# Thirty-six of 72 weight blocks, not 24, get their low part in the first FFN pass of a Mamba and LoRA-FFN layer

## The reference

```python
def lora(x, w, a, b): return x @ w.T + (x @ a.T) @ b.T
mod = (silu(c) @ wmod).reshape(1, 6, 1, -1)       # sa, ca, ga, sb, cb, gb
h = layernorm(x) * (1 + ca) + sa                  # x: 1 x 2048 x 1024, fp32
xp = h @ x_proj_w.T                               # dt_in (32), B (16), C (16)
dt = softplus(dt_in @ dt_proj_w.T + dt_proj_b)
state = exp(dt * A) * state + dt * B * h          # 16 states a channel, over 2048 steps
x = x + ga * (sum(C * state) + D * h)
h = layernorm(x) * (1 + cb) + sb
hidden = silu(lora(h, gate_w, gate_a, gate_b)) * lora(h, up_w, up_a, up_b)   # 2752 wide
x = x + gb * lora(hidden, down_w, down_a, down_b)
```

## Time and profile before

| | us |
|---|---|
| median of 3 runs (2538.43 to 2544.97) | 2539.99 |
| profiled execution | 2542.05 |
| its span, first to last instruction | 2540.3 |
| first phase, to the first matmul of an FFN block | 532.5 |
| pass of chunk 0, 532.5 to 870.7 | 338.2 |
| pass of chunk 1, 870.7 to 1216.9 | 346.2 |

### The profile page before, as it was taken

One profiled execution on the slowest core, in us unless ns is written; L12 is line 12 of the kernel. 1 busy time (PEld: TensorE's weight loads), 2 busy tenths in 40 slices (PEclk: granted clock), 3 DMA queues, 4 the chain that ended last, 5 costly groups with the idle time before them and its releaser, 6 DMA issues.

```text
span 2540.3 us, 34613 instructions
## 1 busy us (share of the span) xinstructions
PE 2139.7 (84%) x11780; PEld 1908.1 (75%) x11780; DVE 1429.3 (56%) x2091; ACT 1439.4 (57%) x2803; POOL 1535.3 (60%) x956
## 2 busy tenths in 40 slices
PE   7446665558787798888899998999989999999999
PEld 4223222257776788887899997899979999999998
DVE  1354344666676567785667775677766777221111
ACT  2554555467685567665667665567656656442332
POOL 0344544689789678676787685786676989210100
PEclk9657667579898899899999999999999999999999
DMA  7554643246776667575666665666757787687786
GB/s 282 160 175 136 229 151 105 83 155 220 243 250 216 202 244 235 198 254 187 239 204 235 227 216 192 226 216 221 236 181 235 250 270 254 216 287 260 252 274 210
DMA packets 156031, 547.89 MB, mean 216 GB/s; under 512 B 17104, under 2 KB 29648, under 8 KB 152784
## 3 DMA queue, kind: packets, MB, share of 16 engines
q1 hardware_dynamic: 155856, 545.68, 64.0%
HBM read 498.32 MB, written 47.30 MB: 215 GB/s over the span
## 4 chain that ended last, share of the span: by engine, by line
PE 49%; DVE 12%; ACT 8%; issue 7%; POOL 4%; DMA 3%; SPq 0%; DVEq 0%; ACTq 0%; POOLq 0%
PE FP L693 43%; DVE ring L1075 6%; PE FP L599 3%; DVE ring L965 2%; POOL ring L1191 2%; ACT whi L902 1%; DMA raw<-w_gu 1%; ACT sqb L872 1%; DMA lo_scratch<-wlo 1%; PE FP L717 1%; DVE FP L1052 1%; POOL y L1164 1%; ACT SC L756 1%; PE FP L656 1%; POOL wlo L1204 1%
## 5 line engine op out<-in xcount | busy, mean ns | idle before, releaser
L1191 POOL TENSOR_TENSOR ring<-ring,c_row 128x736 f32<-128x736 f32 (+2 forms) x384 | 637.0, 1659 | 512.7 <-ACT hst L770 512.2
L756 ACT ACTIVATE SC<-dtb,aneg 128x368 f32<-128x368 f32 (+2 forms) x768 | 415.2, 546 | 670.3 <-DVE ring L1075 660.5
L693 PE MATMUL FP<-xhi,whi 128*128 128x368 f32 (+2 forms) x2160 | 712.1, 330 | 96.9 <-ACT whi L902 23.6
L693 PE MATMUL FP<-xlo,whi 128*128 128x368 f32 (+2 forms) x2160 | 704.4, 326 | 0.0
L693 PE MATMUL FP<-xhi,wlo 128*128 128x368 f32 (+2 forms) x2160 | 704.4, 326 | 0.0
L1075 DVE TENSOR_TENSOR_SCAN ring<-SC,hst,ring 128x368 f32<-128x368 f32 (+1 forms) x640 | 579.8, 948 | 6.8 <-ACT SC L756 6.8
L1164 POOL TENSOR_TENSOR y<-y,ring 128x736 f32<-128x736 f32 (+1 forms) x320 | 555.1, 1735 | 13.8
L693 PEld LDWEIGHTS FP<-xhi,whi 128*128 128x128 f32 x2160 | 422.8, 196 | 109.6 <-ACT whi L902 61.2
L902 ACT ACTIVATE whi<-raw 128x1024 fp32r<-128x1024 f32 (+2 forms) x408 | 409.3, 1010 | 148.2 <-PE FP L717 71.5
L965 DVE TENSOR_TENSOR ring<-hb,SC 128x736 f32<-128x736 f32 (+2 forms) x384 | 328.5, 855 | 223.1 <-PE SC L614 210.4
L693 PE MATMUL FP<-hhi,whi 128*128 128x368 f32 (+5 forms) x1188 | 391.6, 330 | 70.5 <-POOL hlo L1212 42.9
(11 more groups left out here) (97 smaller groups left out, 2355.6 us busy)
## 6 DMA issues: line engine op xcount, KB each, us to landing
wlo<-lo_scratch SPq DMA_DIRECT2D x249, 576.0 KB, 4.3
raw<-w_gu SPq DMA_DIRECT2D x249, 512.0 KB, 4.9
raw<-w_dn SPq DMA_DIRECT2D x107, 448.0 KB, 4.1
wlo<-lo_scratch SPq DMA_DIRECT2D x91, 448.0 KB, 3.9
raw<-w_dn SPq DMA_DIRECT2D x53, 512.0 KB, 4.5
wlo<-lo_scratch SPq DMA_DIRECT2D x51, 512.0 KB, 4.0
raw<-w_gu SPq DMA_DIRECT2D x44, 576.0 KB, 4.5
lo_scratch<-wlo SPq DMA_DIRECT2D x44, 576.0 KB, 5.9
```

The costliest lines, as they stand in the source:

```text
L693: last = mm(out, w, x, start=(start and k == 0 and e == 0), stop=(stop and k == n - 1 and e == 2))
L756: A(SC[:, DA0 + a, 0:CH[c]], tile_of(dtb, c, i), ACT.Exp, scale=aneg[:, i * NS + s:i * NS + s + 1]).then_inc(a_da[a], 1)
L1191: G.tensor_tensor(buf, buf, over_pair(c_row[:, k % C_SLOTS, 0:CH[c]]), ALU.mult).then_inc(g_hc, 1)
```

## The change

One line. `OTF` was each block with u % 3 == 1, 24 of them; now it is each with an odd number, 36. Of the further lists, `PREP` falls from 48 to 36 blocks, and `with_preps` spreads these over the same stretch. Four preparations stand before group 0 of chunk 0 in place of six. By size the low parts formed in the pass were 15 of 1152 columns, 5 of 896, 3 of 1024 and 1 of 560; now they are 22, 8, 4 and 1, and 1 of 640.

```diff
-OTF = [u for u in range(NU) if u % HI_SLOTS == 1]
+OTF = [u for u in range(NU) if u % 2 == 1]
 PREP = [u for u in range(NU) if u not in OTF]
 NPREP = len(PREP)
```

## The result

The changed kernel takes 2559.74 us (median of 4 runs, 2558.97 to 2560.48) against 2539.89; the ratio is 1.0075, 95% interval 1.0057 to 1.0092. It is slower by 19.9 us where 10 were forecast, inside the range of 2532 to 2569. (2539.89 is the median of four runs of the kernel before; the table ahead of the prediction has three of them.)

What follows compares the result with a forecast made beforehand. It took a ring around each scan group to pace the first phase and POOL to bound part of the first FFN pass. The pass 18.8 us longer, first phase 9.1 shorter: net 9.7 longer, 2550 us, range 2532 to 2569.

Steps and rivals of the forecast that it cites:

- First phase: Stretch before the first FFN pass: twelve fewer prepared blocks save ScalarE copies, 9.1 us shorter (bounds 0 to 16.2).
- Among the groups: First phase, scan groups: ten fewer prepared blocks at 0.6 us each, 6.4 us with the copies to extra columns.
- Before group 0: Start of first phase: two fewer prepared blocks, each costing ScalarE its full 1.35 us, save 2.7 us.
- GpSimd's work in the pass: First FFN pass: twelve more low parts, 28.5 us of work, lengthen it by 21.2 us.
- the split by stretches: First FFN pass: added work counted whole in three full stretches (13.9 us), half in the other three (7.3 us).
- SyncE's wait: First FFN pass: a load into a slot waits for the store's landing, 35 times; 2 us in all.
- the wait falls in TensorE's slack: First FFN pass: TensorE starts a loaded unit 2.5 us later but ends it before POOL's next low part.
- Rival (c): First FFN pass: SyncE becomes the bound, deciding from a landing of about 8.3 us; 2571 us; chance 0.16.
- (a): First FFN pass: POOL's waits take in the new work, pass 5 us longer; 2536 us; chance 0.24.
- (b): First FFN pass: TensorE keeps its clock through shorter waits, giving 6 us; 2526 us; chance 0.13.
- Pass 1: Second FFN pass: the later passes hold the same instructions before and after, so no term was given.
- The marks: Signs in the profile: first unit about 523 us, pass 350 to 365, POOL above 88% busy, 35 SyncE waits.

Runs made afterwards that it cites:

- e6: Kernel before with every fourth block's low part formed in the first FFN pass (18 blocks), three slots; 2543.72 us.
- e9: Kernel before with every fourth block's low part formed in the first FFN pass (18) and four slots for low parts; 2517.01 us.
- e7: Kernel before with every sixth block's low part formed in the first FFN pass (12 blocks), three slots; 2542.10 us.
- e12: Kernel before with every sixth block's low part formed in the first FFN pass (12) and four slots for low parts; 2520.25 us.
- e11: Changed kernel with three prepared low parts on VectorE in place of four, the fourth going to GpSimd; 2559.75 us in a single execution.
- e3: Changed kernel whose first-pass stores read a constant tile, so no load waits for a store's landing; 2546.07 us.
- e2: Kernel before with its 24 low parts of the first FFN pass formed over 16 columns only; 2521.79 us.
- e5: Changed kernel with first-pass low parts formed over 16 columns only and their stores reading a constant tile; 2511.79 us.

## Why the prediction was right and where it wasn't

**First phase: -9.1 us forecast, -9.3 measured, with both parts wrong, so the agreement is luck.** Among the groups ten blocks fewer were to give 6.4 us and gave 12.0 (378.1 to 366.1 us) in this pair of traces. Over all traces of the same lists the stretch takes 377.6 to 378.1 us with 41 blocks in it and 366.1 to 369.1 with 31, so 0.9 to 1.2 us a block, up to twice the 0.6 us that I took from the chain's share. Nor is it a price per block: with 45 blocks in the stretch (e6, e9) it takes 374.5 and 374.4 us, less than with 41, and with 50 (e7, e12) 383.6 and 383.9. Where each copy falls among the groups must count as well; that wasn't tested. Before group 0 two blocks fewer were to give 2.7 us, and the first scan came 2.6 us later (101.6 to 104.2). The evenly spread list had moved the fourth block from before the softplus to its middle, and with it VectorE's 1.36 us; e11 shows this. I had costed the move on ScalarE alone, and there it gave nothing: in e11, without those two copies, the scan comes as long after the first copy as in the kernel before.

**GpSimd's work in the pass: 16.8 us forecast** (21.2 for the low parts, 1.1 for ScalarE's, less 5.5 for the store), and e3, which has this alone, is 17.1 us over the kernel before. The sum was right for the work by itself; the split by stretches wasn't tested. The rate of 0.6 us for each us of added work (17.1 of 28.5, the store's 5.5 already taken off) is twice what the first 24 blocks cost (18.3 of 56, e2). The kernels with four slots say the same: 327.8, 334.2, 338.5 and 360.0 us with 12, 18, 24 and 36 blocks formed in the pass, so 10.7 us for the first twelve more and 21.5 for the next.

**SyncE's wait: 2 us forecast, 8.5 us measured beside the whole work, 22.0 without it.** This is the term that made 25.6 out of 18.8. The prediction had its place, its count (35), its landing (7.4 us forecast, 7.5 in the trace of the changed kernel) and the lateness of 2.5 us a pair. The failed step is "the wait falls in TensorE's slack": TensorE stood idle 22.1 us before 13 loaded units whose part had not landed, up to 2.9 us each, and 1.1 us in the kernel before. TensorE's end of a unit is waited for by VectorE and ScalarE, in whose lists the scan stands behind it. VectorE's wait for TensorE before a down block's sum rose from 28.1 to 40.8 us, and is 24.5 us in e3. In the waits in the pass, before and after:

```profile
DVE y L1114 <- PE FP L693: 28.1, 8, 5.9
DVE y L1114 <- PE FP L693: 40.8, 14, 6.2
```

Rival (c) put the danger at a landing over 8.3 us, as a bound of SyncE's queue alone. The medians stayed below that, and yet the landing cost, through the single load that it delays. The prediction had set (c) against the mean pace of the pass. In the stretch from 706.5 to 738 us GpSimd and SyncE were both at their limit; over the whole pass neither was, GpSimd busy for 85.5% of it and SyncE before a landing for 63%.

**Rivals (a) and (b)** fell. GpSimd's idle time was nearly as long as before and its waits for ScalarE rose (48 us after 41), and the granted clock of the pass stayed, 0.88 after 0.89.

**Pass 1** was forecast as untouched and took 3.1 us more (352.1 to 353.0 us in the three traces of that code, 349.7 and 349.9 in the two of the kernel before's). In e3 and e5 it was 8.1 and 5.5 us shorter than in the changed kernel, so the stores at the end of pass 0 may have a part in it; this was not tested.

**The marks.** First unit at 523.3 (523 forecast), pass 364 (350 to 365), 35 low parts with 84.6 us (84), no wait of GpSimd for a store, 35 of SyncE: all as written. A sign of (c), TensorE waiting for loaded low parts, was there too. GpSimd's share was to exceed 88% and was 85.5% (311.6 of 364.3 us), a sign that something besides it held the pass.

## What to carry to other kernels

When a pattern is made denser, look at what shares a buffer slot with what: a period that no longer divides the number of slots turned an unseen wait on one engine into one on the queue that feeds another, and it cost where the delayed load was wanted three units on, and nothing where it was wanted four units on. Two near bounds must be cut together to be priced; cut singly, they showed 8.5 and 22.0 of 44 us. A share of the chain, 0.6 us a copy here, was below what ten copies fewer gave (0.9 to 1.2), and even that was no price per copy. An even respacing moves each copy on every engine, which has to be followed at the start of the stretch too.

## What the runs showed of the hardware

A store of 576 KB to DRAM landed 7.5 us after its issue (median of 22 in the changed kernel's pass) where a load of the same size took 3.8. I had thought that the landing might shorten once nothing was issued behind the store; it stayed at the 7.4 us of the earlier trace rows, while the loads went down from 5.3 to 3.8:

```profile
lo_scratch<-wlo SPq DMA_DIRECT2D x22, 576.0 KB, 7.5
wlo<-lo_scratch SPq DMA_DIRECT2D x22, 576.0 KB, 3.8
```

What else is in flight counts in this: in e3, where store, load and raw loads follow one another without the wait, the medians of the same sizes are 6.7 and 5.8 us, and in the first phase of the changed kernel a store of 576 KB took 5.5.

The Trainium skill (DMA: Bandwidth & Descriptors, section on the anatomy of one DMA), in its account of DMAs issued by GpSimd, says that the final write's confirmation makes most of the fixed cost and is longest when the target is HBM. The direction agrees with the 7.5 against 3.8 us here, which are DMAs issued by SyncE; whether it is the reason wasn't tested, since the store also shares the engines with the raw load issued just ahead of it.
